# A prologue's token table: comparisons shared with GpSimd, products between the experts' weights

## What is computed

```python
def ffn(tgt):                                   # E = 8 experts, F = 512, top 2
    logits = tgt @ Wr.T + br
    top_v, top_i = top_k(logits, 2)
    w = softmax(top_v)
    h = relu(einsum('bsd,efd->bsef', tgt, W1) + b1)
    o = einsum('bsef,edf->bsed', h, W2) + b2
    return layer_norm(tgt + sum_of_two_experts(o, top_i, w), gamma, beta)

x = x + 0.5 * ffn(layernorm(x))
x = x + attention(layernorm(x))
x = x + 0.5 * ffn(layernorm(x))
```

## Time and profile before

| | us |
|---|---|
| median of 3 runs | 646.53 |
| lowest and highest | 645.79, 647.34 |
| the profiled execution | 645.7 |
| its span, first to last instruction | 644.0 |

### The profile page before, as it was taken

How to read it: one execution, slowest core, us unless ns; L and a number is a source line. 1 busy time by engine, 2 the same in 40 slices (tenths; PEclk the granted TensorE clock), 3 DMA queues, 4 the chain that set the end, 5 groups by cost and what they waited for, 6 DMA issues and landing times.

```text
span 644.0 us, 16630 instructions
## 1 busy us (share of the span) xinstructions
PE 583.0 (91%) x4382; PEld 537.3 (83%) x4382; DVE 452.1 (70%) x1421; ACT 446.4 (69%) x1224; POOL 386.9 (60%) x481
## 2 busy tenths in 40 slices
PE   5987999999999788899899899887999999999964
PEld 5887999999999577788797789777989999999831
DVE  5784788446685989699769968976537665467645
ACT  4755666676767577776887696685777777896644
POOL 3007565657667786668515386585775777765633
PEclk9588999999999999899999999999899999999979
DMA  8902233223324210000000001021341423531051
GB/s 259 329 8 58 76 77 71 79 75 89 83 65 80 57 29 17 17 25 18 10 1 0 2 30 36 10 71 31 88 103 57 103 76 97 204 96 40 29 196 66
DMA packets 41882, 45.97 MB, mean 71 GB/s; under 512 B 8726, under 2 KB 32706, under 8 KB 41536
## 3 DMA queue, kind: packets, MB, share of 16 engines
q1 hardware_dynamic: 32496, 27.13, 14.4%
q0 software_dynamic: 9088, 17.75, 10.1%
q10 hardware_dynamic: 208, 0.02, 0.0%
HBM read 25.95 MB, written 19.83 MB: 71 GB/s over the span
## 4 chain that ended last, share of the span: by engine, by line
PE 56%; DVE 20%; ACT 9%; issue 6%; POOL 6%; DMA 1%; ACTq 0%; DVEq 0%; SPq 0%; POOLq 0%
PE banks L1076 20%; PE banks L1086 19%; DVE nb L1841 6%; DVE scratch L1848 3%; PE banks L1069 3%; PE banks L1173 2%; PE banks L964 2%; PE banks L966 2%; PE banks L965 2%; DVE st_r L1338 1%; POOL rows L499 1%; POOL zb L512 1%; DVE mv L1344 1%; ACT tgt L650 1%; POOL rs L480 1%
## 5 line engine op out<-in xcount | busy, mean ns | idle before, releaser
L1076 PE MATMUL banks<-scratch 128*128 128x128 f32 x1248 | 169.1, 279 | 1.8 <-ACT scratch L707 1.3
L1086 PE MATMUL banks<-blocks,scratch 128*128 x1248 | 166.5, 276 | 2.0 <-issue 1.1
L1076 PEld LDWEIGHTS banks<-scratch 128*128 128x128 f32 x1248 | 154.5, 195 | 4.7 <-issue 4.4
L1591 DVE TENSOR_SCALAR scratch<-banks,blocks 128x128 f32<-128x128 f32 x312 | 95.1, 346 | 89.5 <-PE banks L1076 77.5
L1086 PEld LDWEIGHTS banks<-blocks,scratch 128*128 128x128 f32 x1248 | 151.8, 192 | 4.6 <-issue 4.2
L491 POOL DMA_INDIRECT scratch<-xrows,rowbuf x78 | 75.4, 966 | 81.8 <-DVE rowbuf L1486 41.2
L698 ACT ACTIVATE scratch<-banks 128x128 f32<-128x128 f32 x156 | 43.1, 277 | 89.4 <-PE banks L1069 86.9
L789 ACT ACTIVATE scratch<-banks,nb 128x1024 f32<-128x1024 f32 x64 | 71.3, 1115 | 47.6 <-DVE nb L1841 47.2
L524 POOL DMA_INDIRECT results<-scratch,places x78 | 77.8, 998 | 34.4 <-issue 19.7
L714 ACT ACTIVATE scratch<-banks,blocks 128x128 f32<-128x128 f32 x312 | 96.4, 364 | 2.4 <-PE banks L1076 2.1
L707 ACT ACTIVATE scratch<-blocks 128x512 f32 x156 | 97.0, 622 | 0.1
(11 more groups left out here) (265 smaller groups left out, 896.4 us busy)
## 6 DMA issues: line engine op xcount, KB each, us to landing
scratch<-rows SPq DMA_DIRECT2D x78, 64.5 KB, 1.9
yrows<-scratch SPq DMA_DIRECT2D x78, 64.0 KB, 1.5
scratch<-in_L_ffn_W_dram SPq DMA_DIRECT2D x1, 2048.0 KB, 19.8
xrows<-tgt SPq DMA_DIRECT2D x4, 512.0 KB, 4.2
x<-in_L_attn_x_dram SPq DMA_DIRECT2D x3, 512.0 KB, 8.0
scratch<-xrows,rowbuf POOLq DMA_INDIRECT x78, 2.6
results<-scratch,places POOLq DMA_INDIRECT x78, 2.4
rows<-padrows SPq DMA_DIRECT2D x18, 64.5 KB
```

Of the source, the lines that this page charges most:

```text
L1076: ins = pe.matmul(hT_at(T, c), staged(T, c), xT_of(T), start=True, stop=True)
L1086: ins = pe.matmul(y_at(T), hT_of(T, c), blocks[:, W2_AT + c * D:][:, bass.ds(at, D)], start=(c == 0), stop=(c == FC - 1))
L1591: ins = dve.tensor_scalar(hT_of(T, c), hT_at(T, c), blocks[:, B1_AT + c:][:, bass.ds(at, 1)], 0.0, ALU.add, ALU.max)
```

## The change

Four things are moved or given away, and nothing of the computation changes.

1. GpSimd makes the comparisons 16 to 31 of the first pair's 32 (pieces 2 and 3 of 4). It waits for `lo_f` by a new semaphore `lo_ready`, and TensorE waits for these pieces by `low_pool`. VectorE makes pieces 0 and 1. For the second pair VectorE makes all four as before.
2. TensorE runs `find_ids` of the first pair after the weights of six experts, ahead of those of the last two. VectorE runs `pair_index` right after `small_weights`. The gathers wait for 9 pieces of turned weights (the part of `raw1` that the ring covers) instead of all 16.
3. VectorE's `shifts` of batch 1 stands ahead of `router_weights` and `copy_first_turn(0)`.
4. ScalarE writes the first half of batch 1's rows ahead of `copy_tgtT(0, 1)`.

```diff
 def gather_x(T):
-    wait_apart(pool, (idx_ready, T // GSLOTS + 1), (xrows_sent[T // GSLOTS], 16 * GB), (wT_ps, 2 * E))
+    wait_apart(pool, (idx_ready, T // GSLOTS + 1), (xrows_sent[T // GSLOTS], 16 * GB), (wT_ps, 2 * -(-RING * ROW // F) - 1))
...
 # GpSimd, ahead of its first gathers
+            pool.wait_ge(lo_ready, 1)
+            for q in range(2, 4):
+                for i in range(q * IP // 4, (q + 1) * IP // 4):
+                    ins = pool.tensor_scalar(low_at(i), place_b, lo_f[:, i:i + 1], None, ALU.is_equal)
+                ins.then_inc(low_pool, 1)
             for T in range(X_AHEAD):
                 gather_x(T)
...
 # ScalarE
             root(1, (ln_stats, 2))
+            first_rows(1, halves_of(0))
             copy_tgtT(0, 1)
-            for h in range(2):
-                first_rows(1, halves_of(h))
+            first_rows(1, halves_of(1))
...
 # TensorE, find_ids
-                    pe.wait_ge(low_ready, 4 * g + q + 1)
+                    if g == 0 and q >= 2:
+                        pe.wait_ge(low_pool, q - 1)
+                    else:
+                        pe.wait_ge(low_ready, 2 * g + q + 1)
...
 # TensorE
-            weights(range(E))
+            weights(range(E - 2))
+            find_ids(0, range(4))
+            weights(range(E - 2, E))
...
             ins.then_inc(qkT_ps, 1)
-            find_ids(0, range(4))
...
 # VectorE, pair_ids
                 steps.then(dve.tensor_copy(lo_f, lo_i))
+                dve.sem_inc(lo_ready, 1)
...
-            def pair_lows():
+            def pair_lows(g):
-                for q in range(4):
+                for q in range(4 if g else 2):
...
 # VectorE
+            shifts(1, 3).then_inc(ln_rstd, 1)
             router_weights()
             copy_first_turn(0)
-            shifts(1, 3).then_inc(ln_rstd, 1)
...
             small_weights()
+            pair_index(0)
             at_once(pair_weights(0))
             dve.wait_ge(qkT_ps, 1)
             dve.tensor_copy(qkwT[:, :], bank(4)).then_inc(qkT_sb, 1)
-            pair_index(0)
```

More of the change, by code:

```diff
@@ L204, in macaron_kernel @@
         cc_ready, place_sb = sem("cc_ready"), sem("place_sb")
+        lo_ready, low_pool = sem("lo_ready"), sem("low_pool")
         summed, gained, whole = sem("summed"), sem("gained"), sem("whole")
@@ L1936, in _ @@
             at_once(pair_ids(0))
-            at_once(pair_lows())
+            at_once(pair_lows(0))
             small_weights()
+            pair_index(0)
             at_once(pair_weights(0))
@@ L1951, in _ @@
             routing = itertools.chain(pair_choose(1), pair_place(1), pair_table(1), pair_ids(1), pair_weights(1))
-            lows_1 = pair_lows()
+            lows_1 = pair_lows(1)
             for s in range(-2, SLOTS + 1):
```

## The result

The changed kernel takes 651.42 us (median of 4 runs, 650.46 to 652.09), the kernel before 646.16: a ratio of 1.008, 95% interval 1.0063 to 1.0098. It is 5.3 us slower where 2.8 us faster was forecast. The profiled execution took 650.46, its span is 648.7 (644.0 before).

What follows compares the result with a forecast made beforehand. The gather branch before the first tile was taken as the bound. With the M branch deciding afterwards, the first tile moves from 52.39 to 49.6, 2.8 us earlier, taking the median 646.53 to 643.7 us; range 641.8 to 646.3.

Steps and rivals of the forecast that it cites:

- The bound: Ahead of the first tile two branches meet; the gather branch, 2.7 us later than the M branch, decides before the change.
- M's branch: qkw's copy, M's product and its split Ml; not shortened, Ml at 48.35, so it decides after the change.
- Batch 1's shift: Early prologue: moved into an idle hole of VectorE at no cost, it makes all behind it 0.8 us earlier.
- the same low-clock stretch in front: Turning of the experts' weights on TensorE: 4.44 us at granted clock 0.50, as before the change.
- Products between the experts: TensorE's id products after six experts' weights: the sixth's last turn ends at 40.7, the products take about 1.2 us.
- GpSimd's sixteen: GpSimd's 16 comparisons of the first pair: start at 33.9, slip in between VectorE's instructions, end at 41.7.
- I take 0.40: Price in us of one undisturbed GpSimd comparison on 128 columns, set between 0.37 and 0.50.
- I take 41.7: Time in us at which GpSimd's comparisons end, with ten done by 39.2 and bounds of 40.3 and 45.6.
- the stated bound of 45.6: Latest end of GpSimd's comparisons if the two engines never overlap: 33.9 + 5.3 + 6.4 us.
- Behind GpSimd's end: From 41.7: last products 42.1, ScalarE's last copy 44.75, M's product 46.55, Ml 48.35, first tile's product 49.6.
- GpSimd becomes the bound: Rival: comparisons at 0.50 us without overlap end at 47.2, first tile at 55.1, time 649.2 us; chance 0.08.
- The clock stays up: Rival: TensorE keeps its full clock over the first tiles, gain 4.2 us in all, 642.3 us; chance 0.18.

Runs made afterwards that it cites:

- e1_vector_all: The changed kernel with all 32 comparisons on VectorE and none on GpSimd: 645.09 us, ratio 0.9979 against the kernel before.
- e2_shift_only: The kernel before with only batch 1's shift and ScalarE's order of batch 1's first rows changed: 646.21 us, ratio 0.9999.
- e4_kept_busy: The changed kernel plus 30 unread identity turns on TensorE ahead of the last eight id products: 648.9 us, ratio 1.0054 against the kernel before.
- c1_filled: e1_vector_all plus 27 unread identity turns where TensorE waits before the first tile: 643.07 us, ratio 0.9957 against the kernel before.
- e7_prices: The kernel before plus 16 unread GpSimd comparisons in four forms, behind VectorE's 32: 0.60, 0.58, 0.59 and 0.42 us each by form.
- e8_after_ids: The changed kernel with GpSimd's comparisons started behind the last instruction of pair_ids instead of with lo_f: the sixteen took 9.88 us.
- e3: The kernel before with only GpSimd's 16 comparisons added, the products staying behind all eight experts' weights: 648.3 us, ratio 1.0035.
- e6: The changed kernel with 8 comparisons on GpSimd and 24 on VectorE: 776.04 us against 776.73 for the kernel before, ratio 1.0003.
- e10: The kernel of e6 run again, 8 comparisons on GpSimd, on a slow chip: ratio 0.9999 against the kernel before.
- c4: The kernel of e6 run again, where the kernel before takes 646.29 us: 645.4 us, ratio 0.9983.
- e9_filled_again: The kernel of c1_filled, run on a slow chip: 774.83 us against 776.84 for the kernel before, ratio 0.997.

## Why the prediction was wrong

**The bound.** Right: two branches meet ahead of the first tile, and M's branch becomes the later one. The changed kernel's loss was carried through to the second pass. A gain was not wholly: of e1_vector_all's 2.1 us at the first tile 1.2 were left at the second pass, since the low clock over the first tiles lasted 5.1 us and not the 2.8 that I had left unchanged.

**Batch 1's shift.** The hole was there. ScalarE ran batch 1's rows 12.79 to 16.45, and the choice started at 22.72 in an execution whose first 30 turns on TensorE took 0.63 us longer than before, so about 0.8 earlier against its own start. What failed is "the same low-clock stretch in front": the weights were turned at the low clock for 5.9 us (33.48 to 39.4) instead of 4.44, which I had named as a sign of being wrong. In e2_shift_only too the clock rose a microsecond later than before, and the weights ended no earlier. The worth of the shift by itself was measured as 0 with 0.8 just inside the interval.

**Products between the experts.** The order did what it should, 1.1 late: the products could start at 41.80 instead of 40.7, behind the late start of this execution and the longer low clock.

**GpSimd's sixteen.** This is the step that failed and turned the sign: "I take 0.40" and "I take 41.7". Two terms were mis-sized, and the start was 0.7 late (34.57 against 33.9). The price of one undisturbed was 0.58, above the 0.37 to 0.50 that I had bounded it by, because the slope per column came from an iota (1.4 ns) and is 2.6 ns for a comparison; sixteen of those alone are 9.3 us, ending at 43.9. (The 0.40 us for two pointers was itself a mean over disturbed ones: the median of those 32 is 0.34, the longest 0.93.) The disturbance was 2.6 us on top (1.66 and 0.55 for the first two, about 0.1 for each of four). I had assumed one opening at each end of a VectorE instruction, and ten comparisons done by 39.2; the first comparison got none until both parts of L1473 were over, and by 39.2 not four were done. The end came at 46.42 instead of 41.7, past the stated bound of 45.6.

The Trainium skill, Advanced Engine Details and Errata, section VectorE Performance Modes, has GpSimd's instructions and VectorE's two-port ones interfere with and block each other. Here the trace agrees only in part: beside VectorE's bf16 comparisons a GpSimd comparison took 0.68 instead of 0.58, while beside instructions with two SBUF inputs it took 2.24 and 1.13. The Trainium skill, GPSIMD Engine Reference, section Specifications, names both kinds, VectorE's two-port modes and its instructions with two SBUF inputs. In this kernel it is the second that counted. The Trainium skill, GPSIMD Engine Reference, section When to use GPSIMD, advises VectorE for elementwise work, gives GpSimd about twice the time for operations with two inputs, and adds that "1-input is roughly line-rate". The advice was right here and the last figure no guide: this comparison has one input and took 0.58 against VectorE's 0.166, 3.5 times as long. The measurement decides.

**Behind GpSimd's end.** Forecast 7.9 us to the first tile, measured 10.26. The 2.4 lie in five places: the last products 0.76 instead of 0.4; from there to ScalarE's last copy 3.72 instead of 2.65; to M's product 2.13 instead of 1.8 (by its own terms, 2.0 less 0.3, the forecast should have had 1.7); to Ml 2.14 instead of 1.8; to the first product 1.51 instead of 1.25. Most of it follows the granted clock, which fell with the 3.63 us idle stretch that the forecast did not have in its sum: in e4_kept_busy's trace, where it did not fall there, the same way took 8.41, 1.85 less. The other half microsecond, in M's part and the first tile, was there too.

**The rivals.** "GpSimd becomes the bound" is what happened, with its place (in front of the second half of the products, with weights, lambda and M behind) and its turning point: 0.66 us per comparison as the point of no gain, 0.74 measured (11.85 over 16). Its price of a loss came too low: a loss over 0.2% was to start at 0.75 us, and at 0.74 it was 0.8%. Its end of GpSimd's share, 47.2, was 0.8 late and its first tile, 55.1, 1.6 early: the 2.4 us behind GpSimd's end, mostly the clock's, are the difference. Its time of 649.2 was 2.2 short. (The 45.6 that I called this rival's above is the bound of my own term; the rival's end is 47.2.) I gave it 8 in 100, because all of my prices for the one instruction that no row showed came from below, and the full microsecond that L481 was held was argued away by short instructions. "The clock stays up" did not happen in e1_vector_all either; c1_filled made it happen, and it was worth 1.4 (by the ratios) to 2.0 us (by the medians), where 1.4 was the price.

**What is left of the forecast.** Without GpSimd's part the sum said 2.8 less 0.3, and e1_vector_all measured 1.1 to 1.4. Its first tile came 2.1 earlier, near the sum; the rest went in the longer low clock behind it. So the forecast would have been about twice too high even without GpSimd.

## What to carry to other kernels

Before giving an engine a share of the work, price that very instruction on it by a probe: the 0.40 taken from other instructions of that engine was 0.58 here, and sixteen of them made the term. A helper engine whose share ends after the main engine would have finished alone moves the bound, however many instructions it takes off: 16 comparisons cost 6 us, 8 cost and gained nothing measurable. An idle stretch on TensorE such as the 3.63 us here is to be priced with the slow work behind it. Filling such waits with turns that nobody reads brought 0.14% before the change and a further 0.2% in the new order, as much as the moves themselves (0.2%).

## What the runs showed of the hardware that I had not expected

- GpSimd's tensor_scalar with is_equal on 128 x 128: 0.58 to 0.60 us, the same with a pointer or a constant, from bf16 or f32; 0.42 on 64 columns (e7_prices).
- A GpSimd instruction started 0.02 us behind two VectorE instructions with two SBUF inputs (1.53 us in all) took 2.24 us, and 0.79 when it started 0.1 us behind the last instruction of that kind (e8_after_ids). The 2.24 came back in every trace with that start (e3, e4, e6, e10, c4: 2.24 each).
- The eighteen traces, with the same work on TensorE up to there, reached the first normalised rows' turn on TensorE between 11.60 and 12.88 us, with 30 identical turns in front of it taking 5.08 to 6.37 us. The granted clock rose from 0.50 to 1.00 between 36.4 and 40.0 us in sixteen of them and at 30.6 in two, and did not move along with the work. That this makes the scatter of some microseconds that every kernel here shows is likely and not shown.
- On two of the chips every kernel took about 776 us instead of 646, by waits within the tile loop that the profile puts down to "remote" (up to 22 us each; 13 of them hold one line of ScalarE's, L699, for 73 us in e9_filled_again). What they wait for stays open.
